# Reordered attention rounds in a fused attention and mixture-of-experts kernel

## The chip, the cores and the metric

The kernel runs on one core of a Trainium2 chip. The metric is the device time of one execution, in microseconds. Engines: TensorE (PE) multiplies, VectorE (DVE), ScalarE (ACT) and GpSimd (POOL) work on elements, SyncE (SP) issues most DMAs. They run beside one another and wait on semaphores.

## The reference

The input x is 16 x 256 rows of 256 features, 4096 tokens. What is computed, cut to what matters here:

```
v = layernorm(x) @ Wv.T + bv        # 4096 x 128
t = ctx @ Wt.T + bt                 # 4096 x 128, from 192 features
x = x + tanh(g_xattn) * (v . t) / max(|v| |t|, 1e-8)     # per batch entry, 256 x 256
y = layernorm(x)
shared = (silu(y @ w1) * (y @ w2)) @ w3                  # hidden 1024
scores = sigmoid(y @ router_w)                           # 16 experts, top 2 by scores + bias
routed = sum over the two chosen experts of score * swiglu_e(y)   # hidden 256 each
x = x + tanh(g_ffn) * (shared + routed)
```

## The kernel before, in words

The tokens are cut into 8 chunks (NC) of 512 columns; LAST is 7. Everything in the first stage is fp32; for the shared expert each row y is split in two fp16 parts, hi and lo, whose products are added.

The kernel has one instruction stream per engine, written out by hand; each engine runs its own in order. Stages: (1) the text side t and the sums of x, to about 48 us; (2) the attention rounds, one chunk per round, to about 113 us; (3) the shared expert, `hidden(n)` and `late_rows(n)`, while VectorE chooses experts and slots and GpSimd scatters the token table in 64 indirect DMAs; (4) the routed experts by blocks of rows, (5) the rest of the shared expert and the combination.

A chunk c goes through these helpers in the attention rounds:

- TensorE `values(c)` (L1335, L1339): v into bank 5. ScalarE `lead_v(c)` (L622, L625): its squares and its scaled copy VT. TensorE `v_norms(c)` (L1357, eight matmuls one column wide) and `row_norms(c)` (L1349); ScalarE `lead_norm(c)` (L631) takes the root; VectorE `inverse_norm(c)` (L875, L877) clips and inverts it to rv.
- ScalarE `scales(c)` (L640) writes M from rv; TensorE `dots(c)` (L1369) makes the products of v and t in banks 0 and 1; VectorE `attend(c)` (L885) combines the two in M; GpSimd `add_attention(c)` (L518) adds M to X.
- VectorE `statistics2(c)` (L896) and `deviations2(c)` (L904, L907); ScalarE `deviation(c)` (L668); VectorE `normalise2(c)` (L911, L917) writes the scaled rows XL2, which SyncE stores to xrow.
- TensorE `transpose2(c)` (L1382) transposes XL2 into banks 3 and 4; ScalarE `lag(c)` copies each half twice, to X2T in fp32 (L652) and to XHL's hi part in fp16 (L653); GpSimd `cut(c)` (L512) makes the lo part; SyncE stores XHL to xtd.
- TensorE `router(c)` (L1391) multiplies X2T by the router's weights into bank 1; ScalarE `logits(c)` (L659) copies the products; TensorE `router_rows(c)` (L1398) transposes them into bank 7. `dots` of the next round but one writes bank 1 again, so its second half waits for that copy.
- Beside these, a piece of the shared weights is split each round: ScalarE `weights_hi(c)` (L663) and VectorE `weights_lo(c)` (L925), which waits for it.

On ScalarE, VectorE, GpSimd and SyncE the middle rounds are a loop of the engine (`Fori`); on TensorE they are unrolled. The order in each stream sets what can wait for what. SyncE's `store_chunk(c)` waits for XL2 of chunk c and issues its store, then waits for `cut(c)` and issues the store of XHL, 512 KB each:

```
sp.wait_ge(xl2, c + 1)
sp.dma_start(xrow_tiles[:, ds(c * TPC, TPC), :], XL2).then_inc(st_rows, 16)
sp.wait_ge(hl2, c + 1)
sp.dma_start(xtd[ds(c * P, P), :], XHL...).then_inc(st_xt, 16)
```

Behind chunk 2 it fetches chunks 0 and 1 back from xtd into the two halves of XTC (L435), 512 KB each. Stage 3 begins with `hidden(0)` (L1472), behind `transpose2(LAST - 1)`, on three conditions of which two matter here: all eight pieces of `weights_lo`, and the first half of XTC:

```
pe.wait_ge(ws_lo, NC)
pe.wait_ge(v_sq, NC)
pe.wait_ge(vn_sq, NC)
hidden(0, 0, 0, first=True, load=16)      # waits for ld_xtc[0]
```

`router` and `router_rows` of chunk 6, `transpose2(7)` and `router(7)` stand between `hidden(0)` and `hidden(3)`. `deviation(LAST)` stands on ScalarE behind `silu(0)`.

Of the kernel before, what the change touches and what calls it, by code (L numbers as in the profile page):

```python
# [22 lines left out]
def flamingo_block(nc, x, x_t, ctx_t, g_xattn, g_ffn, wv_t, bv, wt_t, bt, router_w, expert_bias,  # L23
# [48 lines left out]
    with ctx:  # L72
# [301 lines left out]
        def _(sp):  # L374
# [56 lines left out]
            with sp.Fori(0, 3) as c:  # L431
                store_chunk(c)
            sp.wait_ge(st_xt, 3 * 16)
# [4 lines left out]
            with sp.Fori(3, NC) as c:  # L438
                store_chunk(c)
# [154 lines left out]
        def _(act):  # L594
# [32 lines left out]
            def lead_norm(c, first=False):  # L627
                act.wait_ge(n_mm, c + 1)
                if not first:
                    act.wait_ge(rv_ready, c)  # L630
                act.activation(vn[:, :], bank[2][:, 0:TPC], ACT.Sqrt).then_inc(vn_sq, 1)  # L631
# [12 lines left out]
            def lag(c, first=False):  # L644
                for u in range(2):
                    act.wait_ge(t2, c * 2 + (u + 1))
                    if u == 0 and not first:
                        act.wait_ge(lt_mm, c)
                        act.wait_ge(hl2, c)
                        act.wait_ge(st_xt, c * 16)  # L650
                    half = bank[3 + u][:, :].rearrange("p (k n) -> p k n", k=KD)
                    act.activation(X2T[:, :, u * D:(u + 1) * D], half, ACT.Copy).then_inc(x2f, 1)  # L652
                    act.activation(XHL[:, 0, :, u * D:(u + 1) * D], half, ACT.Copy).then_inc(x2t, 1)  # L653
# [7 lines left out]
            def weights_hi(c):  # L661

                act.activation(WS[:, 0, ds(c * WP, WP)], SHST[:, ds(c * WP, WP)], ACT.Copy, scale=WSCALE)\  # L663
                    .then_inc(ws_hi, 1)

            def deviation(c):
                act.wait_ge(ve2_ready, c + 1)
                act.activation(sd2[:, :], ve2[:, :], ACT.Sqrt).then_inc(sd2_ready, 1)  # L668
# [23 lines left out]
            deviation(0)  # L692
            act.wait_ge(ld_shared, 48)
            weights_hi(0)
            weights_hi(1)
            scales(1)
            lag(0, True)
            lead_v(2)
            logits(0, bank[1][:, 0:P], True)
            lead_norm(2)  # L700
            deviation(1)
            weights_hi(2)
            with act.Fori(2, LAST) as c:
                scales(c)
                lag(c - 1)
                lead_v(c + 1)
                logits(c - 1, bank[1][:, 0:P])
                lead_norm(c + 1)
                deviation(c)
                weights_hi(c + 1)  # L710
# [129 lines left out]
        def _(dve):  # L840
# [108 lines left out]
            attend(0)  # L949
            statistics2(0)  # L950
            deviations2(0)
            inverse_norm(1)
            normalise2(0, True)
            weights_lo(0)
            with dve.Fori(1, LAST - 1) as c:
                attend(c)
                weights_lo(c)
                statistics2(c)
                deviations2(c)
                inverse_norm(c + 1)  # L960
                normalise2(c)
            weights_lo(LAST - 1)
            attend(LAST - 1)
            statistics2(LAST - 1)
            deviations2(LAST - 1)
            inverse_norm(LAST)
# [322 lines left out]
        def _(pe):  # L1289
# [134 lines left out]
            transpose2(0)  # L1424
            pe.wait_ge(cos_done, 4)
            router(0, bank[1][:, 0:P])
            row_norms(2)
            v_norms(2)

            for c in range(2, LAST):  # L1430
                router_rows(c - 2)
                dots(c, logits=c - 2)
                transpose2(c - 1)
                values(c + 1)
                pe.wait_ge(cos_done, c * 2 + 2)
                router(c - 1, bank[1][:, 0:P])
                row_norms(c + 1)
                v_norms(c + 1)
# [225 lines left out]
```

## Time and profile before

| | |
|---|---|
| time, median of 3 runs | 567.29 us (565.83 to 568.90) |
| span of the profiled execution | 568.1 us |
| TensorE busy | 538.4 us (95%), granted clock 0.973 on average |
| VectorE busy | 399.6 us (70%) |
| ScalarE busy | 307.6 us (54%) |
| GpSimd busy | 270.1 us (48%) |
| chain that ended last | TensorE 68%, GpSimd 14%, VectorE 6%, issue 5%, DMA 4% |

The profiled execution has no time of its own beside its span of 568.1 us, which lies inside the spread of the three runs. The chain goes back from the last instruction to what released each step. A matmul's end is modelled, so neighbouring rows of TensorE overlap by some tenths of a us; the start of the next row is the better mark. "issue" is time in which nothing shown was waited for.

### The profile page before, as it was taken

The numbers are of one execution on the slowest core, as the hardware profiler recorded it, in microseconds if no ns is written. First come the engines' busy times: TensorE is split into PE (matmuls) and PEld (weight loads), VectorE is DVE, ScalarE is ACT, GpSimd is POOL, SyncE is SP. The second block draws the span as 40 slices with busy tenths as digits, with TensorE's granted clock in tenths as the row PEclk, the third lists the DMA queues.
The fourth block names the chain that finished last, engine by engine and source line by source line (L and its number), as shares of the span: only waits on it lengthen the run. The fifth ranks groups of instructions, "written<-read, shape, count | busy, mean of one in ns | idle before, by whom it ended". The sixth has DMA issues, their size and how long they took to land.

```text
span 568.1 us, 13109 instructions
## 1 busy us (share of the span) xinstructions
PE 538.4 (95%) x4164; PEld 348.7 (61%) x4164; DVE 399.6 (70%) x890; ACT 307.6 (54%) x594; POOL 270.1 (48%) x257
## 2 busy tenths in 40 slices
PE   4899799999989999994999999999999999999997
PEld 2467676756556656653566666666666655665664
DVE  1432888867797867772788888888888736677675
ACT  2324666785226665651677777777777733333332
POOL 3001475453417787876443444334443035666770
PEclk9659999999999999997999999999999999999999
DMA  8999626338504120011233333333334123374442
GB/s 223 313 351 310 224 104 222 115 110 284 180 1 152 55 74 20 2 37 35 81 103 105 112 104 109 103 100 113 110 105 107 57 56 104 93 250 121 140 135 88
DMA packets 53228, 72.55 MB, mean 128 GB/s; under 512 B 8032, under 2 KB 43424, under 8 KB 53168
## 3 DMA queue, kind: packets, MB, share of 16 engines
q1 hardware_dynamic: 43984, 51.75, 27.9%
q0 software_dynamic: 8608, 17.91, 11.7%
q10 hardware_dynamic: 576, 2.10, 1.1%
q8 instruction: 37, 0.61, 0.4%
q14 instruction: 23, 0.19, 0.1%
HBM read 49.64 MB, written 22.09 MB: 126 GB/s over the span
## 4 chain that ended last, share of the span: by engine, by line
PE 68%; POOL 14%; DVE 6%; issue 5%; DMA 4%; SPq 1%; ACT 1%; DVEq 0%; POOLq 0%; ACTq 0%
PE bank L1568 17%; PE bank L1472 17%; POOL slot_token L550 12%; PE bank L1493 8%; PE bank L1594 8%; PE bank L1578 4%; PE bank L1308 3%; PE bank L1552 3%; DMA WR<-in_ctx_t 2%; PE bank L1335 2%; PE bank L1297 1%; POOL X L518 1%; DVE STAGE L917 1%; DMA xrow<-STAGE 1%; PE bank L1382 1%
## 5 line engine op out<-in xcount | busy, mean ns | idle before, releaser
L1472 PE MATMUL bank<-XTC,WS 128*128 128x512 f16 x768 | 176.1, 379 | 0.5 <-DVE ROWS L1213 0.5
L1472 PEld LDWEIGHTS bank<-XTC,WS 128*128 128x128 f16 x768 | 74.8, 98 | 78.9 <-issue 1.0
L567 POOL DMA_INDIRECT ROWS<-xrow,idx x72 | 76.8, 1067 | 97.0 <-PE bank L1552 83.7
L1568 PE MATMUL bank<-WR,XTB 128*64 x432 | 100.4, 382 | 0.7 <-DVE STAGE L1219 0.7
L1568 PE MATMUL bank<-STAGE,XTB 128*64 128x512 f16 x432 | 100.4, 382 | 0.0
L584 POOL DMA_INDIRECT ROWS<-yrow,posi x64 | 63.8, 997 | 55.0 <-DMA yrow<-ROWS 26.8
L550 POOL DMA_INDIRECT slot_token<-tokid,sloti x64 | 72.2, 1129 | 34.9 <-issue 19.2
L798 ACT ACTIVATE STAGE<-WR 128x1024 f16 x72 | 76.7, 1066 | 18.2 <-PE bank L1594 17.9
L720 ACT ACTIVATE SIL<-bank 128x512 f32<-128x512 f32 x63 | 37.6, 597 | 81.1 <-PE bank L1472 79.9
L1568 PEld LDWEIGHTS bank<-WR,XTB 128*64 128x64 f16 x432 | 44.7, 110 | 44.1 <-issue 7.7
L1112 DVE SCALAR_TENSOR_TENSOR G<-bank,SIL 128x512 f32<-128x512 f32 x63 | 43.4, 690 | 29.7 <-ACT SIL L720 29.0
L1493 PE MATMUL bank<-WS,GS 128*128 128x256 f16 x516 | 63.2, 273 | 0.0
L1493 PEld LDWEIGHTS bank<-WS,GS 128*128 128x128 f16 x516 | 50.4, 98 | 14.3 <-issue 0.2
L1219 DVE COPY STAGE<-WR 128x2048 f16 x72 | 50.0, 694 | 11.6 <-PE bank L1568 11.3
L518 POOL TENSOR_TENSOR X<-X,WR 128x512 f32 (+1 forms) x16 | 23.6, 1495 | 70.3 <-DVE WR L885 70.3
L1594 PE MATMUL bank<-STAGE,GT 128*64 128x256 f16 x432 | 53.3, 273 | 0.0
L1594 PE MATMUL bank<-WR,GT 128*64 x432 | 53.3, 273 | 0.0
L1594 PEld LDWEIGHTS bank<-WR,GT 128*64 128x64 f16 x432 | 47.1, 110 | 8.0 <-issue 0.8
L1594 PEld LDWEIGHTS bank<-STAGE,GT 128*64 128x64 f16 x432 | 47.1, 110 | 0.0
L727 ACT ACTIVATE GS<-G 128x512 f16<-128x512 f32 x42 | 26.5, 630 | 37.1 <-DVE G L1112 37.1
L785 ACT ACTIVATE SIL<-bank 128x256 f32<-128x256 f32 x72 | 28.3, 393 | 30.5 <-PE bank L1568 30.5
L1568 PEld LDWEIGHTS bank<-STAGE,XTB 128*64 128x64 f16 x432 | 44.7, 110 | 0.0
(171 smaller groups left out, 874.5 us busy)
## 6 DMA issues: line engine op xcount, KB each, us to landing
WR<-in_routed_w SPq DMA_DIRECT2D x39, 256.0 KB, 5.3
yrow<-ROWS SPq DMA_DIRECT2D x72, 128.0 KB, 1.7
X<-in_x SPq DMA_DIRECT2D x4, 1024.0 KB, 13.0
xrow<-STAGE SPq DMA_DIRECT2D x8, 512.0 KB, 2.9
xtd<-STAGE SPq DMA_DIRECT2D x8, 512.0 KB, 2.6
out<-X SPq DMA_DIRECT2D x7, 512.0 KB, 3.3
WR<-in_ctx_t SPq DMA_DIRECT2D x4, 768.0 KB, 10.8
WR<-in_shared_w SPq DMA_DIRECT2D x3, 1024.0 KB, 14.4
```

The source lines that it names most:

```text
L518: pool.tensor_tensor(xs, xs, M[:, 2 * u:2 * u + 2, :], ALU.add).then_inc(added, 1)
L550: pool.indirect_dma_start(out=slot_token, in_=tokid[:, t:t + 1], in_offset=None, out_offset=bass.IndirectOffsetOnAxis(ap=sloti[:, k, t:t + ...
L567: pool.indirect_dma_start(out=XG[:, u, :], out_offset=None, in_=xrow, in_offset=bass.IndirectOffsetOnAxis(ap=idx[:, b:b + 1].bitcast(U32), ...
L584: pool.indirect_dma_start(out=YG[:, u, k, :], out_offset=None, in_=yrow, in_offset=bass.IndirectOffsetOnAxis(ap=posi[:, k, t:t + 1].bitcas ...
L720: act.activation(SIL[:, a, :], HIDDEN[a][0][:, :], ACT.Silu, scale=1.0 / WSCALE).then_inc(s_sil, 1)
L798: act.activation(W3[:, b % 2], odd_half(w, b)[:, :, W3E:WE], ACT.Copy).then_inc(odd_w3, 1)
L1112: dve.scalar_tensor_tensor(out=G[:, a, :], in0=HIDDEN[a][1][:, :], scalar=1.0 / WSCALE, in1=SIL[:, a, :], op0=ALU.mult, op1=ALU.mult).then ...
L1219: dve.tensor_copy(W12[:, b % 2], odd_half(w, b)[:, :, 0:W3E]).then_inc(odd_w12, 1)
L1472: last = pe.matmul(acc[:, :], WS[:, wx, at:at + P], XTC[:, u, xx, k, :], start=(k == 0 and m == 0), stop=(k == KD - 1 and m == 2))
L1493: last = pe.matmul(acc, GATED[n % 3][gx][:, i * P:(i + 1) * P], WS[:, wx, at:at + D], start=(n in (NSE, n - j) and m == 0 and i % 2 == 0), ...
L1568: last = pe.matmul(bank[u][part, :], XTB[:, b % 4, xx, k, part], w[s], start=(k == 0 and m == 0), stop=(k == KD - 1 and m == 2), tile_posi ...
L1594: last = pe.matmul(YB[u][part, 0:D], GT[:, u, gx, k, part], w[s], start=(k == 0 and m == 0), stop=(k == RH // P - 1 and m == 2), tile_posi ...
```

## The change

Within a round the order of each stream changes.

- TensorE: `dots` goes ahead of `router_rows`; `values(c + 1)` goes ahead of `transpose2(c - 1)`; `router(c - 1)` goes last, behind the row norms and v norms. In the opening, `router(0)` goes behind `row_norms(2)` and `v_norms(2)`.
- VectorE: `normalise2` of a chunk moves out of the end of its own round to behind the `attend` of the next. In the opening `weights_lo(0)` stands straight behind `attend(0)`, and `normalise2(0)` behind `attend(1)`.
- ScalarE: `deviation(c - 1)` and `weights_hi(c + 1)` stand behind `scales(c)`, then `lead_v`, `lag`, `lead_norm`, `logits`. Within `lag` both copies to X2T come first, then both to XHL, and the wait for the store of XHL stands only ahead of the latter.
- SyncE: the two fetches of XTC stand behind `store_chunk(5)` instead of `store_chunk(2)`.

No instruction is added or removed.

```
--- before.py
+++ after.py
@@ -428,14 +428,14 @@
             for c in (6, 7):
                 sp.wait_ge(v_mm, c - 5)
                 load_xt(c)
-            with sp.Fori(0, 3) as c:
+            with sp.Fori(0, NC - 2) as c:
                 store_chunk(c)
-            sp.wait_ge(st_xt, 3 * 16)
+            sp.wait_ge(st_xt, 2 * 16)
             for u in range(2):
                 sp.dma_start(XTC[:, u, :, :, :].rearrange("p a k n -> p (a k n)"),
                              xtd[u * P:(u + 1) * P, :]).then_inc(ld_xtc[u], 16)
 
-            with sp.Fori(3, NC) as c:
+            for c in (NC - 2, NC - 1):
                 store_chunk(c)
             sp.wait_ge(st_rows, NC * 16)
             sp.wait_ge(st_xt, NC * 16)
@@ -642,15 +642,17 @@
                     last.then_inc(m_ready, 1)
 
             def lag(c, first=False):
+                halves = [bank[3 + u][:, :].rearrange("p (k n) -> p k n", k=KD) for u in range(2)]
+                if not first:
+                    act.wait_ge(lt_mm, c)
+                    act.wait_ge(hl2, c)
                 for u in range(2):
                     act.wait_ge(t2, c * 2 + (u + 1))
-                    if u == 0 and not first:
-                        act.wait_ge(lt_mm, c)
-                        act.wait_ge(hl2, c)
-                        act.wait_ge(st_xt, c * 16)
-                    half = bank[3 + u][:, :].rearrange("p (k n) -> p k n", k=KD)
-                    act.activation(X2T[:, :, u * D:(u + 1) * D], half, ACT.Copy).then_inc(x2f, 1)
-                    act.activation(XHL[:, 0, :, u * D:(u + 1) * D], half, ACT.Copy).then_inc(x2t, 1)
+                    act.activation(X2T[:, :, u * D:(u + 1) * D], halves[u], ACT.Copy).then_inc(x2f, 1)
+                if not first:
+                    act.wait_ge(st_xt, c * 16)
+                for u in range(2):
+                    act.activation(XHL[:, 0, :, u * D:(u + 1) * D], halves[u], ACT.Copy).then_inc(x2t, 1)
 
             def logits(c, at, first=False):
                 act.wait_ge(lt_mm, c + 1)
@@ -689,25 +691,25 @@
             scales(0, True)
             lead_v(1)
             lead_norm(1)
-            deviation(0)
             act.wait_ge(ld_shared, 48)
             weights_hi(0)
+            scales(1)
+            deviation(0)
             weights_hi(1)
-            scales(1)
+            lead_v(2)
             lag(0, True)
-            lead_v(2)
+            lead_norm(2)
+            weights_hi(2)
             logits(0, bank[1][:, 0:P], True)
-            lead_norm(2)
-            deviation(1)
-            weights_hi(2)
             with act.Fori(2, LAST) as c:
                 scales(c)
+                deviation(c - 1)
+                weights_hi(c + 1)
+                lead_v(c + 1)
                 lag(c - 1)
-                lead_v(c + 1)
+                lead_norm(c + 1)
                 logits(c - 1, bank[1][:, 0:P])
-                lead_norm(c + 1)
-                deviation(c)
-                weights_hi(c + 1)
+            deviation(LAST - 1)
             scales(LAST)
             lag(LAST - 1)
 
@@ -947,23 +949,23 @@
             inverse_norm(0, True)
             dve.wait_ge(clip1_ready, 2)
             attend(0)
+            weights_lo(0)
             statistics2(0)
             deviations2(0)
             inverse_norm(1)
+            attend(1)
             normalise2(0, True)
-            weights_lo(0)
-            with dve.Fori(1, LAST - 1) as c:
+            weights_lo(1)
+            statistics2(1)
+            deviations2(1)
+            inverse_norm(2)
+            with dve.Fori(2, LAST) as c:
                 attend(c)
+                normalise2(c - 1)
                 weights_lo(c)
                 statistics2(c)
                 deviations2(c)
                 inverse_norm(c + 1)
-                normalise2(c)
-            weights_lo(LAST - 1)
-            attend(LAST - 1)
-            statistics2(LAST - 1)
-            deviations2(LAST - 1)
-            inverse_norm(LAST)
             normalise2(LAST - 1)
             weights_lo(LAST)
 
@@ -1422,20 +1424,20 @@
             dots(1)
             values(2)
             transpose2(0)
+            row_norms(2)
+            v_norms(2)
             pe.wait_ge(cos_done, 4)
             router(0, bank[1][:, 0:P])
-            row_norms(2)
-            v_norms(2)
 
             for c in range(2, LAST):
+                dots(c, logits=c - 2)
                 router_rows(c - 2)
-                dots(c, logits=c - 2)
+                values(c + 1)
                 transpose2(c - 1)
-                values(c + 1)
+                row_norms(c + 1)
+                v_norms(c + 1)
                 pe.wait_ge(cos_done, c * 2 + 2)
                 router(c - 1, bank[1][:, 0:P])
-                row_norms(c + 1)
-                v_norms(c + 1)
             dots(LAST, logits=LAST - 2)
             router_rows(LAST - 2)
             transpose2(LAST - 1)
```

## Rows read from the trace of the kernel before

**Rows 1.** The page, part 4: the chain that ended last, share of the span by engine.

```profile
PE 68%; POOL 14%; DVE 6%; issue 5%; DMA 4%; SPq 1%; ACT 1%; DVEq 0%; POOLq 0%; ACTq 0%
```

**Rows 2.** Timeline of GpSimd: start, us, instruction, [idle before <-releaser].

```profile
79.05 1.27 POOL L518 TENSOR_TENSOR X<-X,WR 128x512 f32 x1 [3.15 <-DVE WR L885]
...
108.24 2.12 POOL L512 TENSOR_TENSOR STAGE<-STAGE 128x1024 f16<-128x1024 f32 x1
...
168.52 1.16 POOL L550 DMA_INDIRECT slot_token<-tokid,sloti  x1 [15.73 <-DVE sloti L1066]
```

**Rows 3.** Timeline of TensorE: its long waits at the start and later.

```profile
16.87 2.32 PE L1308 MATMUL bank<-WR,wt 96*128 96x512 f32 x4 [2.41 <-DMA WR<-in_ctx_t]
...
266.93 0.66 PE L1552 MATMUL bank<-ident,ROWS 128*128 128x128 f32 x2 [7.95 <-DMA ROWS<-xrow,idx]
```

**Rows 4.** Busy time by stretch: one round of the loop.

```profile
core 0: us, PE busy (x) PEld busy (x) DVE busy (x) ACT busy (x) POOL busy (x), PEclk, DMA share, GB/s
...
75.90:84.40 8.50, 8.20 (x65) 6.37 (x64) 7.22 (x22) 5.96 (x15) 5.30 (x3) 1.00 0.34 125
```

**Rows 5.** Timeline of TensorE: opening, last dots, first shared step.

```profile
61.00 1.04 PE L1382 MATMUL bank<-ident,STAGE 128*128 128x128 f32 x8
...
63.36 0.64 PE L1391 MATMUL bank<-STAGE,rw 128*32 128x128 f32 x16 [1.32 <-ACT STAGE L652]
...
65.99 1.95 PE L1369 MATMUL bank<-WR 128*128 128x256 f32 x8
...
69.62 1.09 PE L1382 MATMUL bank<-ident,STAGE 128*128 128x128 f32 x8 [1.69 <-DVE STAGE L917]
...
110.12 1.97 PE L1369 MATMUL bank<-WR 128*128 128x256 f32 x8
...
113.35 2.75 PE L1472 MATMUL bank<-XTC,WS 128*128 128x512 f16 x12
```

**Rows 6.** Timeline of ScalarE: opening, and the last copy of chunk 5.

```profile
52.47 1.57 ACT L640 ACTIVATE WR<-bank,rv 128x256 f32<-128x256 f32 x4 [0.89 <-PE bank L1349]
...
56.76 0.17 ACT L631 ACTIVATE vn<-bank 128x4 f32<-128x4 f32 x1 [0.57 <-PE bank L1357]
...
58.69 1.56 ACT L663 ACTIVATE WS<-WR 128x768 f16<-128x768 f32 x2
...
106.33 0.62 ACT L653 ACTIVATE STAGE<-bank 128x512 f16<-128x512 f32 x1
```

**Rows 7.** Timeline of VectorE, and weights_lo by line (ns min/median/max).

```profile
53.45 0.87 DVE L885 SCALAR_TENSOR_TENSOR WR<-WR,clip,bank 128x256 f32<-128x256 f32 x2 [1.46 <-ACT WR L640]
...
57.05 0.75 DVE L896 BATCH_NORM_STATS2 st<-X 128x6 f32<-128x256 f32 x2 [0.49 <-POOL X L518]
...
58.67 0.18 DVE L877 RECIPROCAL rv<-vn 128x4 f32<-128x4 f32 x1
...
59.03 1.38 DVE L917 TENSOR_SCALAR STAGE<-X,mv,rs 128x256 f32<-128x256 f32 x4
...
67.05 0.56 DVE L907 TENSOR_SCALAR ve<-mv 128x4 f32<-128x4 f32 x1
...
67.52 0.16 DVE L875 TENSOR_SCALAR vn<-vn 128x4 f32<-128x4 f32 x1
...
94.17 1.39 DVE L917 TENSOR_SCALAR STAGE<-X,mv,rs 128x256 f32 x4 [0.59 <-DMA xrow<-STAGE]
...
L925 DVE SCALAR_TENSOR_TENSOR WS<-WR,WS x8: 950/1573/1590, 60.3 to 112.3; - x5, 128x768 f16<-128x768 f32 x3
```

**Rows 8.** Timeline of SyncE: the first halves are fetched.

```profile
87.16 0.83 SPq L435 DMA_DIRECT2D XTC<-xtd  x2
```

**Rows 9.** By line, L435: issue to landing of the two fetches.

```profile
DMA to landing us min/median/max: 3.4/4.3/5.2
```

**Rows 10.** Busy time by stretch, columns as in rows 4.

```profile
18.40:18.60 0.20, 0.20 (x2) 0.07 (x1) 0.00 (x0) 0.00 (x0) 0.00 (x0) 0.50 1.09 348
...
270.80:271.00 0.20, 0.20 (x4) 0.06 (x2) 0.00 (x0) 0.20 (x1) 0.15 (x1) 0.55 0.57 143
```

## The prediction

> **What bounds the kernel now.** I read the shares of the chain that ended last first, then its pieces in order of time, then the timeline of each engine over the attention rounds, then TensorE's waits and the granted clock. The chain [rows 1] is mostly TensorE, but 14% of it lies on GpSimd: the table's indirect scatter, which starts at 168.5 us, when VectorE has the slots [rows 2]. TensorE later stands idle 7.95 us for the first gathered rows [rows 3]. So the shared expert's steps beside the scatter have room, and what counts is the time at which the slots are ready. Between `hidden(0)` at 113.35 us and that moment TensorE's contiguous work and VectorE's routing chain lead one another, so a shift of `hidden(0)` arrives at the end of the kernel one for one. The question is when `hidden(0)` starts.
>
> Ahead of it the eight attention rounds run. In a round of 8.50 us TensorE is busy 8.20 us, at full clock [rows 4]. The gap of 0.3 us is the wait of the transposes for VectorE's scaled rows. The opening has larger ones: 1.32 us before `router(0)` and 1.69 us before `transpose2(1)` [rows 5]. From `dots(2)` at 65.99 to `dots(7)` at 110.12 us five rounds take 44.1 us. So the whole stake of the reordering is a few us in 567.
>
> **Opening.** VectorE now has `weights_lo(0)` straight behind `attend(0)`. It needs `weights_hi(0)`, which ScalarE issues behind `lead_norm(1)`, ending at 56.93 us; the pair of `weights_hi` took 1.56 us, so one is done at 57.7 [rows 6]. Before, `statistics2(0)` ran at 55.8 to 57.8. Now: `weights_lo(0)` 57.85 to 58.7 (0.95 with its tail), statistics 1.4 (0.75 for two) to 60.1, and from the end of the statistics to the end of the reciprocal of v's norms as before, 57.80 to 58.85, 1.05: 61.15 [rows 7]. Only then can ScalarE scale for round 1. From its start to `attend` took 0.98 us (52.47 to 53.45), with 0.2 for the hop: `attend(1)` at 62.3, 1.6 us long (0.87 for two). Only behind it stands `normalise2(0)`: 0.2 for its reciprocal, 1.3 for the rows, done at 65.4. The transposes of chunk 0 start at 65.5 instead of 61.00. TensorE has nothing to pass it with, since the row norms stand behind them: 4.5 us idle. Then transposes 1.0, and router, row norms and v norms 2.4 (63.36 to 65.99 less the 0.25 us of `router_rows`): `dots(2)` at 68.9, 2.9 us late. The 1.32 us gap is gone in that.
>
> **Rounds.** TensorE's work alone is 8.1 to 8.2 us a round [rows 4]. VectorE's ring is now, from one `attend` to the next, in us: attend 1.6; reciprocal to rows 0.3; rows 1.3; `weights_lo`; statistics 1.4; to the aggregate 0.15; aggregate 0.4; then 0.47 from `ve` to `vn` as inside the loop (67.05 to 67.52), not 0.1 as I take it outside (57.80 to 58.67 holds all three steps); 0.2 and 0.18 for the reciprocal; 1.2 for the scales and the hop. That is 7.2 without `weights_lo`. Before, the scales' 1.2 us lay beside `normalise2`; now nothing does. `weights_lo` took 0.95 us alone and 1.57 when GpSimd's addition had begun before it [rows 2, 7]. The two additions of 1.27 us each now start 1.1 us after `attend` and end at 3.6, `weights_lo` is reached at 3.2 and done at 4.4, so it costs 1.2 with its wait. Sum 8.4. TensorE waits 0.3 us a round as before; only its place changes. The first round, which TensorE leads, takes 8.1, four take 8.4: 41.7 against 44.1, a gain of 2.4. `dots(7)` starts at 110.6, 0.5 us late. ScalarE is no bound: its products' copy has the first half of `dots` to hide behind, and its X2T copies find the cut of the last round done. If that cover were gone, each costs at most its own 0.5 us a round.
>
> The stall of `normalise2` on a row store, behind the two fetches of the first halves, was one of 0.59 us inside those 44.1 [rows 7]; its removal is in the 8.4.
>
> The scaled rows now run beside GpSimd's additions, which no row of before shows. Bounds: nothing, if they don't collide, and per round up to what `weights_lo` lost, 0.6, plus one addition, 1.3. I take nothing: four scaled rows take 1.38 us, which is little under twice the two-input pair of `attend`, 0.87 [rows 7], so nothing in them shows a doubled pace or a second input. The Trainium skill (SBUF — State Buffer, section "Who interferes with whom") says that a VectorE instruction with two SBUF inputs, or a `tensor_scalar` in a 2-port mode, and a GpSimd one lock each other out for their whole length. The 1.57 against 0.95 agrees for two inputs. For the scaled rows the rule speaks against the change, if they run in such a mode; by the pace of the row they don't.
>
> **End.** `transpose2(6)` comes at 112.9 (rows scaled behind the same ring), and TensorE would reach `hidden(0)` at 113.9. But `hidden(0)` needs the first half of XTC. Before, the fetches were issued at 87.16 us, 26 us ahead of need, and took 3.4 to 5.2 us to land [rows 8, 9]. Now they stand on SyncE's queue behind `store_chunk(5)`, whose second part waits for the cut of chunk 5. That cut needs the hi parts of chunk 5, which ScalarE writes last. `attend(6)` comes 1.8 us behind `dots(6)` (the way over norms and scales), at 104.1; its round scales the rows until 3.2, transposes them from 3.3, and the two X2T and two hi copies of 0.5 us each follow from 4.0: 6.1 us after `attend(6)`, 110.2 (before, they were done at 106.95 [rows 6]). With 0.15 for the hop and 2.12 for the cut (it ended at 110.36 before [rows 2]) it ends at 112.4. The store of it is issued at 112.5, the first fetch at 112.9. It lands at 116.3 with the 3.4 us of before, and later if the 512 KB store ahead of it is still moving, to which I give 0.6: 116.9. `hidden(0)` starts 3.6 us late, of which 3.0 is this new wait. Behind the fetches on SyncE's queue nothing is lost: chunks 6 and 7 are stored later than before by the same few us, and the expert loads behind them have 7.95 us of room. Nor does the rest absorb the shift: `silu(0)`, two table loads and the last chunk's rows all hang on `hidden(0)` itself.
>
> **Clock.** TensorE's granted clock fell to 0.50 (1.2 GHz) 1.5 us after a gap of 2.41 us with thin matmuls before it. It was at half speed too when work came back after the 7.95 us gap, and rose only at 270.98, after 4.1 us of it [rows 3, 10]. After the gaps of 1.32 and 1.69 us it stayed at full speed. The new gap of 4.5 us is longer than one that cost the clock, so I expect a fall. Price: at least the 2.05 us lost in those 4.1; at most, if `row_norms`, `v_norms` and `router` run at half speed and the return comes only in `values(3)`, about 4. I take 3, between them. In this case nothing absorbs it but 0.3 us.
>
> **Sum.** Opening +2.9, rounds -2.4, fetch +3.1 over that, clock +3: +6.6. The profiled execution's span of 568.1 us is 0.8 above the median of the runs, 567.3, inside their spread; on the median that gives 573.9.
>
> **Rivals.**
> 1. The clock holds through the gap: +3.6, 570.9. For it: both falls in the trace may have needed more than idleness of this length. Chance 0.25.
> 2. It falls twice, in the opening and again in the 3 us before `hidden(0)`: +3.6 +3 +2.5, 576.4. Chance 0.12.
> 3. The scaled rows and the additions lock each other out: 0.45 to 1.7 us in five rounds, 2.3 to 8.5, some +5 on rival 1: 576. The pace of the row speaks against it. Chance 0.06. This is the case of the Trainium skill's rule, if the mode is the 2-port one.
> 4. Not slower: TensorE's own pace rules everywhere. The place is VectorE's ring; from 8.1 us downward it no longer decides. If the opening also loses nothing (transposes of chunk 0 by 62.7), `dots(7)` starts at 66.0 + 5 x 8.1 = 106.5. The cut of chunk 5 then ends 1.8 later at 108.3, the fetch is issued at 108.9 and lands at 112.6 (3.4, and half of the 0.6), 0.7 us before the old start: 566.6. Even here the fetch ends last; were it not to, 109.5 and 563.5. Chance 0.17 for all of this, a third of it faster by more than 0.5%.
>
> **How the numbers follow.** The forecast has 0.40. No change that this kernel's measurement can tell is within 0.5%, 2.8 us: 564.5 to 570.1. Faster 0.06; within, two thirds of rival 4 and the low edge of rival 1, 0.18; slower 0.76. The range takes rival 1 with an error of 2 us below and rivals 2 and 3 above: 568 to 577.5. The forecast's own is 571.5 to 576.5.
>
> **What would show it.** Opening: an idle of 4 to 5 us on TensorE before the first transposes, released by VectorE's scaled rows, and `dots(2)` near 69. Clock: a stretch at 0.50 between 65 and 80 us. Rounds: `dots` to `dots` 8.4 us, the gap now between values and transposes. End: an idle of about 3 us before `hidden(0)`, released by the fetch of XTC. Port: scaled rows longer than 0.41 us. The forecast is wrong if TensorE doesn't wait for XTC, or if the gap of the opening is under 2 us.

## The result and the profile after

The changed kernel takes 593.15 us (592.1 to 595.31, 4 runs) against 568.10 us (565.83 to 572.13) for the kernel before: ratio 1.0413, interval 1.0379 to 1.0446. Slower was right; the size was not: 6.6 us over the median then shown were forecast, 25 came, and the range ended 16 us too low. The profiled execution's span is 593.6 us against 568.1. All ratios here compare fast runs alone; the profiled executions of E5, E6 and E8 were slow ones, in which the instructions of the stage read here keep the lengths that they have in the others. The shares of its chain hardly differ from [rows 1]:

```profile
PE 67%; POOL 13%; DVE 6%; issue 6%; DMA 4%; ACT 1%; SPq 1%; DVEq 0%; POOLq 0%; ACTq 0%
```

So the shares don't tell where the time went. TensorE's timeline does: start, us, instruction, and in brackets the idle time before it and what ended it. After, `dots` is L1371, the transposes L1384, the row norms L1351, `hidden` L1474; the rows answer to [rows 5]:

```profile
67.69 1.97 PE L1384 MATMUL bank<-ident,STAGE 128*128 128x128 f32 x8 [5.29 <-DVE STAGE L919]
69.45 1.62 PE L1351 MATMUL bank<-ident,rt 128*128 128x128 f32 x8
...
72.36 1.99 PE L1371 MATMUL bank<-WR 128*128 128x256 f32 x8
...
79.52 1.09 PE L1384 MATMUL bank<-ident,STAGE 128*128 128x128 f32 x8 [2.33 <-DVE STAGE L919]
...
84.40 3.61 PE L1371 MATMUL bank<-WR 128*128 128x256 f32 x8
...
94.93 1.99 PE L1371 MATMUL bank<-WR 128*128 128x256 f32 x8
...
102.63 1.09 PE L1384 MATMUL bank<-ident,STAGE 128*128 128x128 f32 x8 [2.87 <-DVE STAGE L919]
...
105.91 1.99 PE L1371 MATMUL bank<-WR 128*128 128x256 f32 x8
...
118.44 3.65 PE L1371 MATMUL bank<-WR 128*128 128x256 f32 x8
...
128.91 1.99 PE L1371 MATMUL bank<-WR 128*128 128x256 f32 x8
...
132.59 1.09 PE L1384 MATMUL bank<-ident,STAGE 128*128 128x128 f32 x8 [1.52 <-DVE STAGE L919]
136.73 5.28 PE L1474 MATMUL bank<-XTC,WS 128*128 128x512 f16 x12 [3.05 <-DMA XTC<-xtd]
```

`dots(2)` starts at 72.36 instead of 65.99, `dots(7)` at 128.91 instead of 110.12, `hidden(0)` at 136.73 instead of 113.35. The five rounds took 12.04, 10.53, 10.98, 12.53 and 10.47 us: 56.55 against 44.13. The loss is in the rounds, where a gain had been forecast. VectorE's timeline over the third of them, which ran at full clock, behind one line of the opening (`attend` L887, scaled rows L919, `weights_lo` L927, the clip of v's norms L877):

```profile
65.00 2.63 DVE L919 TENSOR_SCALAR STAGE<-X,mv,rs 128x256 f32<-128x256 f32 x4
...
94.34 0.17 DVE L909 TENSOR_SCALAR ve<-mv 128x4 f32<-128x4 f32 x1
94.77 1.99 DVE L877 TENSOR_SCALAR vn<-vn 128x4 f32<-128x4 f32 x1 [0.26 <-ACT vn L631]
96.79 0.18 DVE L879 RECIPROCAL rv<-vn 128x4 f32<-128x4 f32 x1
98.14 1.66 DVE L887 SCALAR_TENSOR_TENSOR WR<-WR,clip,bank 128x256 f32<-128x256 f32 x4 [1.17 <-ACT WR L640]
99.71 0.17 DVE L913 RECIPROCAL rs<-sd 128x4 f32<-128x4 f32 x1
100.24 2.33 DVE L919 TENSOR_SCALAR STAGE<-X,mv,rs 128x256 f32 x4 [0.36 <-DVE rs L913]
102.49 0.94 DVE L927 SCALAR_TENSOR_TENSOR WS<-WR,WS  x1
```

and GpSimd's over the same time (the cut L512, the additions L518):

```profile
64.30 2.54 POOL L518 TENSOR_TENSOR X<-X,WR 128x512 f32 x2 [6.17 <-DVE WR L887]
...
94.60 2.13 POOL L512 TENSOR_TENSOR STAGE<-STAGE 128x1024 f16<-128x1024 f32 x1 [4.12 <-ACT STAGE L655]
...
99.20 2.57 POOL L518 TENSOR_TENSOR X<-X,WR 128x512 f32 x2 [2.47 <-DVE WR L887]
```

Two VectorE instructions have grown. The scaled rows take 2.33 instead of 1.38 us while the additions run (99.20 to 101.77). And the clip, 512 numbers, takes 1.99 instead of 0.16 to 0.17 us: it starts 0.17 us behind the cut and ends with it, at 96.7. Over the five rounds the rows take 2.33, 2.12, 2.33, 2.33 and 2.02 us, the clips 1.51, 0.81, 1.99, 1.99 and 0.86: both lose less in the two rounds whose matmuls were slow. The wait lies inside the instruction's own duration, so no view of waits shows it.

The granted clock of TensorE by stretch (columns as in [rows 4]); it was 1.00 in the round of [rows 4]:

```profile
60.00:66.00 6.00, 2.40 (x12) 1.43 (x10) 4.76 (x18) 3.46 (x8) 1.70 (x2) 1.00 0.56 201
66.00:70.00 4.00, 2.31 (x11) 2.31 (x12) 3.85 (x9) 0.90 (x2) 0.84 (x1) 0.65 0.31 106
...
80.00:84.00 4.00, 4.00 (x34) 3.95 (x36) 2.39 (x11) 2.24 (x5) 1.54 (x1) 0.61 0.39 131
...
88.00:94.00 6.00, 5.18 (x37) 4.04 (x35) 5.34 (x13) 2.83 (x6) 2.22 (x2) 1.00 0.22 75
...
118.00:121.00 3.00, 3.00 (x18) 2.17 (x11) 1.22 (x3) 2.25 (x7) 0.67 (x1) 0.50 0.43 175
138.00:140.00 2.00, 2.00 (x6) 0.72 (x5) 0.00 (x0) 0.00 (x0) 0.83 (x1) 0.50 0.51 185
```

In this stage and at its end the clock fell four times: in the opening, in the rounds that began at 72.36 and 105.91, and at `hidden(0)`, whose twelve matmuls took 5.28 instead of 2.75 us. SyncE's queue and the landing of the two fetches, which answer to [rows 8, 9]:

```profile
130.86 0.34 SPq L426 DMA_DIRECT2D xtd<-STAGE  x1
131.41 1.10 SPq L435 DMA_DIRECT2D XTC<-xtd  x2
```

```profile
DMA to landing us min/median/max: 5.2/5.6/6.1
```

### The profile page after: what moved, and what is told of

The parts are those of the page before. It is cut to its first block, busy times and chain, and to the rows that moved or that the text cites. A ratio compares the mean times of both kernels' runs of the same rounds, so it can differ in the third digit from the quotient of the medians.

```text
span 593.6 us, 13117 instructions
## 1 busy us (share of the span) xinstructions
PE 549.9 (93%) x4164; PEld 357.3 (60%) x4164; DVE 407.4 (69%) x890; ACT 308.7 (52%) x594; POOL 267.7 (45%) x257
## 4 chain that ended last, share of the span: by engine, by line
PE 67%; POOL 13%; DVE 6%; issue 6%; DMA 4%; ACT 1%; SPq 1%; DVEq 0%; POOLq 0%; ACTq 0%
PE bank L1474 17%; PE bank L1570 16%; POOL slot_token L550 12%; PE bank L1495 8%; PE bank L1596 8%; PE bank L1580 3%; PE bank L1310 3%; PE bank L1554 3%; DMA WR<-in_ctx_t 2%; PE bank L1371 2%; PE bank L1299 1%; PE bank L1384 1%; PE bank L1351 1%; PE bank L1359 1%; POOL X L518 1%
## 5 line engine op out<-in xcount | busy, mean ns | idle before, releaser
L1474 PE MATMUL bank<-XTC,WS 128*128 128x512 f16 x768 | 178.6, 383 | 3.6 <-DMA XTC<-xtd 3.0
L1474 PEld LDWEIGHTS bank<-XTC,WS 128*128 128x128 f16 x768 | 75.3, 99 | 83.6 <-issue 7.0
L518 POOL TENSOR_TENSOR X<-X,WR 128x512 f32 (+1 forms) x16 | 20.3, 1284 | 69.1 <-DVE WR L887 69.1
```

What stands on the lines that cost most here:

```text
L1474: last = pe.matmul(acc[:, :], WS[:, wx, at:at + P], XTC[:, u, xx, k, :], start=(k == 0 and m == 0), stop=(k == KD - 1 and m == 2))
```

## The experiments

E kernels are edits of the changed one, P and V of the one before, M kernels measure single instructions. "Stage" is the time from `dots(0)` to the start of `hidden(0)` in the trace: 64.74 us before (48.61 to 113.35), 86.88 after (49.85 to 136.73). From E4 on, runs come from chips on which the kernel before itself took 625 or 645 us, with the excess behind this stage; there the stage and the ratios count, not the microseconds. From `hidden(0)` to the end P1's trace has 497 us and E7's 534, against 455 before and 457 after; what makes that excess isn't known, and a shift of `hidden(0)` need not arrive there one for one. E5 and E8 leave out most of the attention besides, so their ratios don't price the stage.

**E1: the clip left out.**

```
-                dve.tensor_scalar(vn[:, :], vn[:, :], TINY, None, ALU.max).then_inc(rv_own, 1)
-                dve.wait_ge(rv_own, c + 1)
```

> The changed kernel without the clip of v's norms at 1e-30 (128x4, one tensor_scalar per round) ahead of their reciprocal; the clip is left out of the computation. Theory P: the clip waited for the end of GpSimd's cut, 1.99 against 0.17 us, in five rounds and the opening, with the way over the scales behind it. Taking it out makes a warm round 9.1 us instead of 10.98 and leaves gaps of about 1 us, in which TensorE's clock holds in the rounds: the time falls by 9 to 13 us, to 580 to 584. Rival C (the loss is TensorE's half clock alone, and the waits fill what it leaves): the rounds are set elsewhere, and the time falls by less than 2 us.

Ratio 1.0309 (1.0271 to 1.0347) instead of 1.0413, some 6 us; stage 79.7; a round of 9.42 us (`dots` at 91.89 and 101.31) instead of 10.98. The clip's wait is real, but 1.56 us a round came back, not 1.8; neither the 9.1 us nor the 580 to 584 us expected were reached (586.41). ScalarE's timeline shows what is next, the copy of the router's products (L661) ahead of the scales (L640):

```profile
101.45 0.28 ACT L661 ACTIVATE LTS<-bank 128x128 f32<-128x128 f32 x1 [0.43 <-PE bank L1391]
101.89 1.57 ACT L640 ACTIVATE WR<-bank,rv 128x256 f32<-128x256 f32 x4 [0.17 <-issue]
```

The reciprocal was done at 101.32, but `router` stands last on TensorE now, so the scales wait for its copy.

**E2: the fetches back behind chunk 2.**

```
-            with sp.Fori(0, NC - 2) as c:
+            with sp.Fori(0, 3) as c:
```

> The changed kernel with the first halves of XTC fetched behind chunk 2 again. Theory: the 3.05 us wait before hidden(0) goes, and with it the 2.6 us that hidden(0) lost at half clock, while a row store may again delay one round by up to 0.6: 3 to 5.5 us less than the changed kernel, 587.5 to 590. Rival: something else is ready as late as the fetch (the last pieces of weights_lo, or the rows of chunk 6), and the time falls by under 1 us.

Ratio 1.0333 (1.0285 to 1.038), some 4.5 us back. `hidden(0)` follows the transposes without a wait and takes 2.75 us; stage 84.1, so 2.8 us of it. The fetch's late place costs its wait and, through the clock, the slow `hidden(0)`.

**E3: VectorE's old order (rows scaled at the end of their own round) with the other engines' new one.**

```
                 attend(c)
-                normalise2(c - 1)
                 weights_lo(c)
...
                 inverse_norm(c + 1)
+                normalise2(c)
```

and on ScalarE `deviation(c)` behind `lead_norm(c + 1)`, ahead of `logits`. In the opening `weights_lo(0)` goes back behind `normalise2(0)`, and ScalarE's `weights_hi(1)` ahead of `scales(1)`.

> The changed kernel with VectorE's order of before (rows scaled at the end of their own round), and ScalarE's deviations where that needs them; TensorE's order, lag and the late fetch stay. Theory P: the scales' way lies beside the scaled rows again and the rows no longer meet the additions, but the clip and the rows can now meet the cut, which comes later than before: if they do, a round takes 9 to 10 us and the time is 577 to 584; if they miss it, a round is TensorE's own 8.1 and the time is 566 to 571 with the fetch's wait. Rival N (TensorE's new order is itself the loss): the time stays within 3 us of the changed kernel's 593.

582.53 us, ratio 1.0228 (1.0195 to 1.026), stage 74.95: VectorE's order, with these places on ScalarE, is worth 12 us of it. The rounds now alternate between 7.88 and 10.2 to 13.1 us. The long ones have this row:

```profile
89.92 1.10 PE L1371 MATMUL bank<-WR 128*128 128x256 f32 x4 [2.06 <-ACT LTS L661]
```

My placing made that: `deviation` waited 2.41 us for `ve` (of which 0.37 are `ve` itself meeting the cut, 0.54 us instead of 0.17), and the copy stood behind it. So E3 bounds the share of VectorE's order from below; E7 mends it.

**M1: twelve instruction forms, each alone and then beside a GpSimd subtraction of the cut's size.** The core of it:

```
pool.tensor_tensor(GL[:, :], GA[:, :], GH[:, :], ALU.subtract)     # 128x1024, 2.12 us
dve.tensor_scalar(OUT[:, 0:256], IN[:, 0:256], SC[:, 0:1], SC[:, 1:2], ALU.subtract, ALU.mult)
```

> This kernel leaves out all of the computation: it copies x to the output, and beside that VectorE runs twelve forms of instruction, each once with GpSimd idle and once started just after GpSimd began a subtraction of 128x1024 elements with two inputs in SBUF (2.1 us in the kernel). Theory P (the two engines lock each other out of a shared port): tensor_scalar from SBUF to SBUF, clip of 128x4 and rows of 128x256 alike, takes up to 2 us longer in the second case, since it waits for the end of the subtraction; so do the two-input form with both inputs in SBUF and the copy. Reciprocal, bn_stats, and every form with PSUM on one side take the same time in both. Rival Q (the lengthening in the changed kernel comes from something else, such as waiting on X, which both engines touch, or a slow semaphore): all twelve take the same time in both cases.

The form of the scaled rows gave a clear answer in VectorE's timeline, alone and beside:

```profile
6.24 0.41 DVE L57 TENSOR_SCALAR OUT<-IN,SC 128x256 f32<-128x256 f32 x1 [2.22 <-POOL GL L90]
6.80 2.35 DVE L57 TENSOR_SCALAR OUT<-IN,SC 128x256 f32<-128x256 f32 x1
```

The second ends with GpSimd's subtraction (6.89 to 9.01), whose record starts 0.09 us after it. In every form of M1 VectorE's record starts some 0.1 or 0.2 us ahead of GpSimd's. The forms with scalars from memory (this one and the one of 255 columns) were held even so; the clip, the form with immediates, the one with two inputs from SBUF and the copy kept their time, and the last three show in GpSimd's subtraction, which took 2.18, 2.31 and 2.18 us instead of 2.12. So M1 doesn't settle the clip, and M2 repeats all forms.

**E4: the cut made short** (8 of 512 columns, the lo part of the others is left out), the additions as they are.

```
+pool.tensor_tensor(XHL[:, 1, :, 0:8], X2T[:, :, 0:8], XHL[:, 0, :, 0:8], ALU.subtract)
```

> The changed kernel with GpSimd's cut shortened to 8 of 512 columns; the lo part of the other columns is left out (zero). The clip stays. Theory P (the clip only waited for the cut): as without the clip, a warm round is 9.4 us instead of 10.97 and the time falls by 6 to 9 us. Rival D (what helped was one instruction less on VectorE, whatever GpSimd does): a round stays over 10.5 us and the time within 2 us of the changed kernel.

Rounds of 9.42 us in steady state, as forecast and as in E1, rows still 2.33, clip 0.17; stage 78.1. That two ways of freeing the clip give one round is the evidence that it was the cut it waited for. (The times give no ratio, so the 6 to 9 us expected can't be told from them.)

**E5: the additions made short as well** (8 of 256 columns; most of the attention is left out).

```
+xs = X[:, ds(c * TPC + 2 * u, 2), 0:8]
+pool.tensor_tensor(xs, xs, M[:, 2 * u:2 * u + 2, 0:8], ALU.add)
```

> As the one before, and GpSimd's additions shortened to 8 of 256 columns too; most of the attention is left out of x. Theory P: the scaled rows take 1.4 us again instead of 2.33 and the statistics wait for nothing, so VectorE's ring is the 8.4 of the prediction and TensorE's gap is under 0.6 us; the opening's gap falls from 5.3 to about 4 us. The time falls by another 5 to 7 us, to 12 to 16 below the changed kernel; what is left over before is the opening and the late fetch. Rival L (the scales' way, and ScalarE's products' copy ahead of it, is what sets the ring, not the ports): a round stays above 9 us, and this kernel is within 2 us of the one with the short cut alone.

Rows 1.38 us again, round 8.46, stage 69.97. The ratio is 0.9832 (0.9721 to 0.9943), under 1 although the stage is 5.2 us longer than before: something outside the stage is faster in it, and what that is was not looked for. The gap of the opening is 4.05 instead of 5.29. VectorE, then ScalarE, in one round:

```profile
97.78 1.38 DVE L921 TENSOR_SCALAR STAGE<-X,mv,rs 128x256 f32 x4 [0.36 <-DVE rs L915]
```

```profile
93.56 0.17 ACT L633 ACTIVATE vn<-bank 128x4 f32<-128x4 f32 x1
94.17 0.28 ACT L663 ACTIVATE LTS<-bank 128x128 f32<-128x128 f32 x1 [0.43 <-PE bank L1395]
94.62 1.57 ACT L642 ACTIVATE WR<-bank,rv 128x256 f32<-128x256 f32 x4 [0.17 <-issue]
```

The ring is read from these: scales at 94.62, `attend` at 95.67, rows 97.78 to 99.16, transposes at 99.22, row norms, v norms, `router`, its copy, scales at 103.08: 8.46. It goes through all three engines.

**E6: weights_lo(0) behind the norms of the opening instead of ahead of the statistics.**

```
             attend(0)
-            weights_lo(0)
             statistics2(0)
             deviations2(0)
             inverse_norm(1)
+            weights_lo(0)
```

> The changed kernel with one instruction moved: weights_lo(0) behind inverse_norm(1) instead of ahead of statistics2(0). Theory O: VectorE's 2.3 us wait for weights_hi(0) no longer lies ahead of the statistics, the first transposes start 2.3 to 3 us earlier, and TensorE's gap of 5.3 us is about 2.5, so that its clock may hold: 2.5 to 5 us less than the changed kernel. Rival: the gap is set by attend(1) and the scaled rows alone, and the time stays within 1 us.

The gap is 3.12 instead of 5.29, and the transposes of chunk 0 start 15.67 us after `dots(0)` instead of 17.84 (12.39 before): 2.2 us back, just under the 2.3 to 3 expected. The clock, which I had hoped would hold, fell all the same, and the stage is 84.5. The times give no ratio either.

**P1: the kernel before with the fetches behind chunk 5, nothing else.**

```
-            with sp.Fori(0, 3) as c:
+            with sp.Fori(0, NC - 2) as c:
```

> The kernel before with the late fetch alone. The cut of chunk 5 ends at 110.4 us in it, so the first fetch is issued at about 110.9 and lands at 114.3 or later, against 113.35: 1 to 1.7 us lost, 0.46 won back where no row store waits behind the fetches: 0 to 1.5 us over before. Rival: the fetch needs the 4 to 5 us that it needed under load, and 2 to 3.5 us are lost, with TensorE's clock 5.

The fetches are issued at 110.39, and TensorE waits:

```profile
116.00 4.17 PE L1472 MATMUL bank<-XTC,WS 128*128 128x512 f16 x12 [3.17 <-DMA XTC<-xtd]
```

Stage 67.57, 2.8 more, and 1.4 more in `hidden(0)` at the fallen clock. Ratio 1.0099 (0.999 to 1.0208), which doesn't exclude that nothing was lost. In the trace my expectation of 0 to 1.5 us was too low and its rival held; the forecast's 3.0 for the wait was right. The rounds behind the first take 8.50 us, the last 8.25, where one had taken 8.96: the stall on the row store [rows 7] is gone, as the forecast had it, and gives 0.46 back.

**V1: the kernel before, without the two small instructions that can meet the cut.** The two `tensor_scalar` on 128x4 go: the floor and the epsilon become biases of ScalarE's two square roots. SyncE issues the row store of chunk 3 ahead of the two fetches instead of behind them.

```
+act.activation(vn[:, :], bank[2][:, 0:TPC], ACT.Sqrt, bias=floor[:, 1:2])
+act.activation(sd2[:, :], mv2[:, :, 1], ACT.Sqrt, bias=floor[:, 0:1])
```

> A version meant to beat both: the order of before, with the two small tensor_scalars of a round (the clip of v's norms and the addition of epsilon to the variance, each exposed to GpSimd's cut) replaced by a bias inside ScalarE's square roots, and the two fetches of XTC issued behind the row store of chunk 3 instead of ahead of it. From v_norms to the scaled rows the way is 0.2 us shorter, and the variance no longer waits 0.4 us for the cut; TensorE's gap of 0.3 us closes, and the store's stall of 0.46 us goes: a round takes 8.1 to 8.3 us and the time falls by 1.5 to 3 us (0.3 to 0.5%), at the edge of what the rounds can tell. Rival: VectorE's loop, with weights_lo locked out by the addition, holds the round at 8.5 and nothing changes.

Ratio 0.9946 (0.9902 to 0.9991): faster than the kernel before by half a per cent. A steady round takes 8.41 instead of 8.51, and the 8.1 to 8.3 expected was not reached. The trace doesn't show where the gain comes from: its stage is 66.97 us, 2.2 longer than before. More than that lies in the round of `dots(2)`, 12.95 instead of 9.90 us, where the clock fell after a gap of 3.06 us and the rows of chunk 1 waited 2.13 us for the store of chunk 0's rows, issued behind expert loads. On VectorE:

```profile
63.95 1.38 DVE L922 TENSOR_SCALAR STAGE<-X,mv,rs 128x256 f32 x4 [2.13 <-DMA xrow<-STAGE]
```

**E7: E3 with the copy of the products ahead of deviation.**

```
                 lead_norm(c + 1)
-                deviation(c)
                 logits(c - 1, bank[1][:, 0:P])
+                deviation(c)
```

> The changed kernel with VectorE's old order, as run before, but with ScalarE's copy of the router's products ahead of the deviation. It tells whether the 7.4 us that TensorE waited for that copy came from the place that I had given it behind the deviation. Theory: yes; those waits go, hidden(0) starts 4 to 7 us earlier than in that run, and what is left is the clip's wait for the cut in the rounds in which they meet. Rival: the clip's wait alone makes the rounds of 9.9 us, and hidden(0) starts within 2 us of that run.

Stage 70.44 instead of 74.95. Of the waits for the copy one is left, 3.29 us in the opening, where `deviation(1)` still stands ahead of it; three middle rounds take 8.19 to 8.26 us (`dots` at 85.62, 93.81, 102.07, 110.33). Ratio 1.0061 (1.0013 to 1.0109). So with rows scaled at the end of their round, the new orders of TensorE and ScalarE run a quarter of a us a round faster than before, and VectorE's order accounts for up to 16.4 of the 22.1 us. The long waits of this trace are the fetch's 3.13, the copy's 3.29, and 2.53 before `transpose2(6)`. Its rows took their usual 1.38 us; `ve` ahead of them met a cut (0.63 us), which is 0.46 of the 2.53.

**E8: everything named so far mended in the changed kernel** (short cut and additions, early fetches, the opening of E6).

> The changed kernel with short additions and a short cut (most of the attention and of the lo part left out), weights_lo(0) behind inverse_norm(1), and the early fetch. If the causes are complete and add up, from dots(0) to hidden(0) it takes what it took with short additions and cut (70.0 us), less the wait for the fetch (2.9) and 2.2 for the opening: 64 to 66 us, against 64.7 in the kernel before and 86.9 in the changed one; the time is within 3 us of before. Rival: a cause is missing, and the stage stays above 68 us.

Round 8.46, gap of the opening 0.84, stage:

```profile
47.06 1.97 PE L1373 MATMUL bank<-WR 128*128 128x256 f32 x8
...
109.38 2.75 PE L1476 MATMUL bank<-XTC,WS 128*128 128x512 f16 x12
```

62.3 us, 2.4 under the kernel before, at full clock, and under the 64 to 66 expected. The opening gave 4.6 us over E5 instead of 2.2: its gap fell from 4.05 to 0.84, since with short additions the statistics wait for nothing either, and with the clock held another 1.4 came back. So the named causes cover the 22 us of the stage. It is no fair race against the kernel before, which keeps its full cut and additions and their collisions; a small cause that the short cut and additions hide as well isn't excluded. Ratio 0.9868 (0.9792 to 0.9944).

**M2: M1 with VectorE started surely behind GpSimd's instruction** (two writes to PSUM ahead of each form).

> The kernel of single forms again (it leaves out all of the computation), with VectorE held back by two fills of PSUM, so that GpSimd's subtraction has been running for about 1 us when the form starts. Theory P: the clip of 128x4, the rows with scalars from SBUF and with immediates, the two-input form and the copy, all from SBUF to SBUF, last about 1 us longer than alone; reciprocal, statistics, and the forms with PSUM on one side last as long as alone. Rival: only instructions of 256 elements or more are held up.

VectorE's timeline, each form alone and beside (the clip L56, the rows L57, with immediates L58, rows written to PSUM L60, the clip read from PSUM L62, the reciprocal L63):

```profile
3.53 0.17 DVE L56 TENSOR_SCALAR OUT<-SC 128x4 f32<-128x4 f32 x1 [0.94 <-POOL GM L85]
...
5.18 0.97 DVE L56 TENSOR_SCALAR OUT<-SC 128x4 f32<-128x4 f32 x1
6.24 0.41 DVE L57 TENSOR_SCALAR OUT<-IN,SC 128x256 f32<-128x256 f32 x1
...
8.13 1.02 DVE L57 TENSOR_SCALAR OUT<-IN,SC 128x256 f32<-128x256 f32 x1
9.19 0.29 DVE L58 TENSOR_SCALAR OUT<-IN 128x256 f32<-128x256 f32 x1
...
10.97 1.03 DVE L58 TENSOR_SCALAR OUT<-IN 128x256 f32<-128x256 f32 x1
...
17.01 0.55 DVE L60 TENSOR_SCALAR PO<-IN,SC 128x256 f32<-128x256 f32 x1
...
22.65 0.16 DVE L62 TENSOR_SCALAR OUT<-PS 128x4 f32<-128x4 f32 x1
...
25.29 0.18 DVE L63 RECIPROCAL OUT<-SC 128x4 f32<-128x4 f32 x1
```

and GpSimd's first instruction of the series:

```profile
4.01 2.12 POOL L90 TENSOR_TENSOR GL<-GA,GH 128x1024 f16<-128x1024 f32 x1 [0.51 <-DVEq L103]
```

The clip starts at 5.18 and ends at 6.15, with GpSimd's 6.13. The rows with scalars from memory and with immediates, an odd length of 255, a copy (1.03 instead of 0.29), and two inputs from SBUF (1.16 instead of 0.43) are held too and end 0.14 to 0.3 us behind GpSimd's. Whatever has PSUM on one side keeps its time (0.55, 0.54, 0.16, 0.48), as do the reciprocal (0.18) and the statistics (0.43). Each form was run once.

## Why the prediction failed

In the traces, `hidden(0)` starts 23.4 us later and takes 2.5 longer, 25.9; the spans differ by 25.5. By the terms of the sum:

| term | forecast | measured |
|---|---|---|
| start of the rounds' stage, `dots(0)` | 0 | +1.2 (varies between runs) |
| opening, to `dots(2)` | +2.9 | +5.1 |
| five rounds | -2.4 | +12.4 |
| `dots(7)` to `hidden(0)` | +3.1 | +4.6 |
| clock | +3 | +2.5 in `hidden(0)`; some 1.4 and 1.7 lie in the two terms above |

**The step that failed** is the sum of VectorE's ring, 8.4 us: it prices two instructions as if GpSimd stood still, the scaled rows at 1.3 and the clip at 0.2. A round measured 10.98; the rows cost 0.95 of the difference and the clip 1.56. For the rows the failed step is "The scaled rows now run beside GpSimd's additions ... I take nothing". I reasoned from pace: at 1.38 us for four, the rows showed no doubled pace. M1 and M2 show that the inference is void: the same form takes 0.41 us alone, which is the pace of the trace, and still waits to the end of GpSimd's instruction. The rule that I had quoted from the Trainium skill (SBUF — State Buffer, "Who interferes with whom"), a lock for the whole length of the instruction, agrees with 1.02 and 2.35 us for 0.41 beside a subtraction of 2.12. The section names `tensor_scalar` among the operations that can take the shared pair; what I took for its exception, the mode, can't be read off a duration. Price: 0.95 us in three of the five rounds, 0.74 and 0.64 in the other two, and 1.25 in the opening. The rounds' part, 4.2, is inside the 2.3 to 8.5 of rival 3, which was this mechanism and had 0.06. What it lacked was the second place; its total of 576 was 17 us short.

**The collision that I did not look for**, the clip's, is worth more. The v norms now stand behind the transposes of their round, as the cut does by way of the hi copies. So the clip arrives when the cut has just begun, and waits 1.8 us in the rounds at full clock. E1's stage, without it, is 7.2 us shorter. I had its evidence in hand: `ve`, of the same shape, takes 0.56 us at 67.05 in [rows 7], and I booked that, and the step behind it, as overhead of the loop. Before, on VectorE and on GpSimd, in the next round:

```profile
75.36 0.57 DVE L907 TENSOR_SCALAR ve<-mv 128x4 f32<-128x4 f32 x1
76.12 0.17 DVE L875 TENSOR_SCALAR vn<-vn 128x4 f32<-128x4 f32 x1 [0.20 <-ACT vn L631]
```

```profile
73.77 2.12 POOL L512 TENSOR_TENSOR STAGE<-STAGE 128x1024 f16<-128x1024 f32 x1
```

`ve` ends when the cut does, 75.9. A 128x4 instruction that took 0.17 us in one place and 0.57 in another was the lock, visible before the change; with it the rule for the rows would have been settled too. The same trace shows the lock the other way round: GpSimd's second addition takes 1.99 instead of 1.27 us where VectorE's `weights_lo` holds it up.

**The rounds add up.** E5's ring is 8.46. The rows add 0.95. The clip adds 1.82 less the 0.26 by which the scales had waited for the copy of the products anyway (94.62 less 94.25, the reciprocal's end, less the 0.11 of the hop after). That is 10.97; the warm round took 10.98. Five make 54.85. The 1.7 up to 56.55 is what the clock's falls cost net: 12.04 and 12.53 us in the two rounds in which it fell, and 10.53 and 10.47, less than 10.97, in the two behind them.

**The ring's size was right and its path was not.** I summed a ring on VectorE and ScalarE, 8.4; E5 and E8 show 8.46. But it closes over TensorE's transposes, norms and `router` and over the copy of its products, which I had called covered by the first half of `dots`. The copy had cover against `dots`, and none against the scales behind it on ScalarE. That the two agree within 0.1 is partly chance.

**Right steps.** In the opening `weights_lo(0)` waits for ScalarE (2.27 us of idle on VectorE, started at 58.93; forecast 57.85, in a stage that began 1.2 earlier) and the gap is 5.29 against a forecast of 4.5; E5's 4.05, with rows of 1.38, is the like-for-like figure, and E6 shows that the place of `weights_lo(0)` makes 2.2 of it. The shift arrived at the end one for one, 25.9 at the end of `hidden(0)` and 25.5 in the span. The late fetch costs a wait of 3.05 (forecast 3.0; P1: 3.17). Two errors cancelled there: the fetch was issued 2.3 us ahead of TensorE's arrival, at 131.41, not 1.0, and landed after 5.2, not 4.0. The stall on the row store went, as P1 shows. The clock fell in the opening, as forecast, but that cost 1.4 us (4.67 from the transposes to `dots(2)`, against 3.28 in E8), not 3. That it would fall again I had at 0.12 and for `hidden(0)` alone; it fell in two rounds more, behind gaps of 2.33 and 2.87 us that the lock had lengthened.

**Left open.** How much of the change's loss a real reordering could save was not tried: E7 with the early fetches would be the next kernel. By its terms it would stand near 67.3 us of stage, still over 64.7, as long as the opening's wait for the copy stays.

## What to carry to other kernels

Before moving a VectorE instruction, list what GpSimd does in the stretch it leaves and in the stretch it enters, and take every scale, clip and copy from SBUF to SBUF, however small, as held to the end of GpSimd's instruction, until the trace shows it beside one at its usual time (GpSimd's here all read two inputs from SBUF). Read unequal durations of one shape as a possible wait, not as overhead, and compare their ends with the other engine's: a small instruction in a ring costs what it can collide with. And when a producer is put last on one engine, look at what stands behind its consumer on the next.

## What the runs showed of the hardware

- The lock between VectorE and GpSimd holds for a clip of 128x4 (0.17 to 0.97 us), and its time stands inside the held instruction's duration. With PSUM as source or target an instruction kept its time, and so did the reciprocal and the statistics (M2, one run of each form; in the kernel before two statistics of 74.04 kept 0.75 us beside the cut of 73.77).
- GpSimd is held as well: an addition of 128x512 took 1.99 us instead of 1.27 beside VectorE's `weights_lo` (before), the subtraction of 2.12 us took 2.31 beside a two-input form that had begun first (M1).
- A `tensor_scalar` of 128x256 in fp32 took 0.41 us with scalars from memory and 0.29 with immediates, and was held in both forms.
- Of two rounds alike, with gaps of 2.87 us before the transposes, one kept full clock (102.63) and one fell to 0.50 (113.60). E1's rounds, with gaps of 1.3 to 1.4 us, all kept it. A round at the fallen clock cost little over a warm one where VectorE led (12.04 and 12.53 against 10.98), since the slower matmuls filled the gap.
- Two 512 KB fetches issued right behind a 512 KB store took 5.2 and 6.1 us to land, against 3.4 and 5.2 for the same two after other traffic [rows 9].
